# Similarity attention of layer 2: one run of intermediate products in front, then one block of eight groups with block-diagonal products

## The reference

```python
def _L2_gnn_ref(matrix, mask, adj, W):
    intermediate = jnp.einsum('bsh,hd->bsd', matrix, W)
    similarities = jnp.einsum('bsd,btd->bst', intermediate, matrix)
    similarities = similarities * adj
    key_mask = mask[:, None, :].astype(bool)
    masked = jnp.where(key_mask, similarities, NEG_INF)
    attn = jax.nn.softmax(masked, axis=-1)
    output = jnp.einsum('bst,bth->bsh', attn, matrix)
    return output
...
x = x + _L2_gnn_ref(_layernorm(x, axis=-1), nodemask, adj, L2_gnn_W)
```

## Time and profile before

| | us |
|---|---|
| median of 3 executions | 3874.0 (3872.6 to 3877.59) |
| the profiled execution | 3859.76 |
| its span, first to last instruction | 3857.9 |
| PE busy, PEld busy | 3137.0, 1980.1 |
| DVE busy, ACT busy, POOL busy | 2420.5, 1336.8, 234.5 |
| mean granted clock of PE, as a share of full speed | 0.871 |

### The profile page before, as it was taken

One profiled execution on the slowest core, in us unless ns is written; L12 is line 12 of the kernel. 1 busy time (PEld: TensorE's weight loads), 2 busy tenths in 40 slices (PEclk: granted clock), 3 DMA queues, 4 the chain that ended last, 5 costly groups with the idle time before them and its releaser, 6 DMA issues. The chain is left out here.

```text
span 3857.9 us, 56708 instructions
## 1 busy us (share of the span) xinstructions
PE 3137.0 (81%) x21385; PEld 1980.1 (51%) x21385; DVE 2420.5 (63%) x4174; ACT 1336.8 (35%) x2519; POOL 234.5 (6%) x196
## 2 busy tenths in 40 slices
PE   6357999999999999535549995789885988986998
PEld 5224555555555555324426663556552655653665
DVE  6636767777767776399673334488895345773333
ACT  3223434344434344110434443312111444543444
POOL 0000000000000000000000000033221004320000
PEclk7678999999999999755769997699997987897999
DMA  3121121112111112100013321000000212102322
GB/s 38 48 82 37 37 51 37 37 38 59 37 40 48 37 37 51 46 13 1 29 32 78 78 55 15 5 1 0 1 0 26 69 39 51 41 22 58 75 68 68
DMA packets 145000, 152.62 MB, mean 40 GB/s; under 512 B 66628, under 2 KB 124896, under 8 KB 142328
## 3 DMA queue, kind: packets, MB, share of 16 engines
q1 hardware_dynamic: 144800, 149.72, 16.0%
HBM read 141.26 MB, written 8.44 MB: 39 GB/s over the span
## 5 line engine op out<-in xcount | busy, mean ns | idle before, releaser
L812 DVE TENSOR_TENSOR f_hg<-f_hs,f_gb 128x640 f32<-128x640 f32 x320 | 263.7, 825 | 507.6 <-ACT f_hs L794 448.5
L2278 PE MATMUL hy_ps<-hy_uT,hy_win 128*128 128x512 f32 x1152 | 498.7, 594 | 0.0
L794 ACT ACTIVATE f_hs<-f_ph,f_b1t 128x320 f32<-128x320 f32 x640 | 335.1, 527 | 406.2 <-PE f_ph L762 402.2
L762 PE MATMUL f_ph<-XNP,f_w 128*128 (+1 forms) x1280 | 404.8, 440 | 12.9 <-PEq L644 8.6
L777 PE MATMUL f_po<-f_hg,f_w 128*128 128x320 f32 x1280 | 404.9, 439 | 8.9 <-DVE f_hg L812 8.9
L2278 PEld LDWEIGHTS hy_ps<-hy_uT,hy_win 128*128 128x128 f32 x1152 | 217.6, 190 | 281.2 <-issue 281.2
L762 PEld LDWEIGHTS f_ph<-XNP,f_w 128*128 128x128 f32 x1280 | 247.3, 194 | 117.5 <-issue 18.8
L777 PEld LDWEIGHTS f_po<-f_hg,f_w 128*128 128x128 f32 x1280 | 240.4, 191 | 126.4 <-issue 21.3
L2338 PE MATMUL hy_ps<-hy_wo,hy_yg 128*128 128x512 f32 x512 | 227.4, 603 | 0.0
L1803 PE MATMUL er_c<-XNG 128*128 128x400 f32 x544 | 204.6, 516 | 22.4 <-POOL XNG L1734 22.1
L1748 ACT ACTIVATE er_OT<-er_t 128x384 bf16<-128x384 f32 x128 | 61.1, 490 | 309.1 <-PE er_t L1773 309.1
(11 more groups left out here) (520 smaller groups left out, 5506.6 us busy)
## 6 DMA issues: line engine op xcount, KB each, us to landing
f_gb<-gate_rows SPq DMA_DIRECT2D x32, 1280.0 KB, 8.5
XNG<-hy_decays SPq DMA_DIRECT2D x32, 1024.0 KB, 9.5
hy_rb<-hy_inverse SPq DMA_DIRECT2D x128, 128.0 KB, 3.1
f_gb<-gate_rows SPq DMA_DIRECT2D x16, 640.0 KB, 5.1
g_KB<-g_keys SPq DMA_DIRECT2D x32, 320.0 KB, 4.5
hy_xn<-XNP SPq DMA_DIRECT2D x1, 4096.0 KB, 12.5
hy_XC<-hy_xn SPq DMA_DIRECT2D x16, 256.0 KB, 3.4
XNG<-in_L_ffn_edge_index_dram SPq DMA_DIRECT2D x2, 2048.0 KB
```

Source lines behind the costliest of these rows:

```text
L762: pe.matmul(psh[e % 2][k][:], w1[:, e, k * 128:(k + 1) * 128], chunk_view(g, c), start=True, stop=True).then_inc(h_ps, 1)
L794: ins = act.activation(hs[:, e % 2, k, :], psh[e % 2][k][:], ACT.Gelu, bias=b1t[:, e * H2 + k:e * H2 + k + 1])
L812: dve.tensor_tensor(hg[:, e % 2], hs[:, e % 2], gb[:, par, e, None, :].broadcast_to([128, H2, CH]), ALU.mult).then_inc(hg_ready, 1)
L2278: mm = pe.matmul(p[:], win[:, t, m * 128:(m + 1) * 128], uT[:, t, :], start=(t == 0), stop=(t == KT - 1))
```

## The change

The two blocks become one. The mask's 0/1 factor is multiplied into a product of mask and adjacency once (`key * adjG`), so that one multiplication out of PSUM applies both. PE makes all 16 intermediate products first, only their 320 real columns, and ACT keeps all of them in `inter` (128 x 128 x 40). Then PE, ACT and DVE go through eight groups of two chunks (`GC` = 2): in round k PE makes the scores of group k and, for group k - 2, turns the attention and makes the output products; DVE works out the softmax of group k in two parts (`shift`, `scale`) and between them adds the outputs of group k - 2 to `XT`. The turned tiles of a pair are copied to a block-diagonal `PT` (zeroed once by POOL), so that one product over 128 rows and 80 columns serves both graphs of a pair. The score products load 40 columns of weights in place of 64; the partitions in between are zeroed once in PSUM. The program of `l2_gnn` after the change (lines taken away are left out):

```diff
 
 def l2_gnn(nc, g):
 
+    GC = 2
+    GROUPS, GQ = NCH // GC, GC * CHP
     with nc.cleanup_on_exit(), ExitStack() as ctx:
         sb = lambda s, shape: ctx.enter_context(nc.sbuf_tensor(f"g2_{s}", shape, F32))
         sem = lambda s: nc.alloc_semaphore(f"g2_{s}")
...
+        w, inter = sb("w", [D, D]), sb("inter", [128, B, N])
         P, key, hide, st = sb("P", [128, PAIRS, N]), sb("key", [128, PAIRS, N]), sb("hide", [128, PAIRS, N]), sb("st", [128, PAIRS])
...
+        PT = sb("PT", [128, 2, CHP, 2, N])
+        bank = lambda s, shape: ctx.enter_context(nc.psum_tensor(f"g2_{s}", shape, F32))
+        psi, pss = [bank(f"i{i}", [128, CH]) for i in range(2)], [bank(f"s{i}", [128, CHP, N]) for i in range(2)]
+        pst, psz = [bank(f"t{j}", [128, CHP, N]) for j in range(2)], [bank(f"z{i}", [128, CH]) for i in range(2)]
+        w_in, key_in, blank, i_ps, i_out, s_ps, s_out, shifted, expd, attn, t_ps, t_out, z_ps, z_out = map(sem, (
+            "w_in", "key_in", "blank", "i_ps", "i_out", "s_ps", "s_out", "shifted", "expd", "attn", "t_ps", "t_out", "z_ps", "z_out"))
         block = ctx.enter_context(nc.Block())
+        group = lambda k: range(k * GC, (k + 1) * GC)
+
+        @block.sync
+        def _(sp):
+            sp.dma_start(w[:], g.L2_gnn_W).then_inc(w_in, 16)
+            masks = g.nodemask.rearrange("(q j) m -> j q m", j=2)
+            for j in range(2):
+                sp.dma_start(key[SLOT * j:SLOT * (j + 1), :, :], masks[j][None, :, :].broadcast_to([SLOT, PAIRS, N])).then_inc(key_in, 16)
+
+        @block.gpsimd
+        def _(pool):
+            pool.memset(PT[:], 0.0).then_inc(blank, 1)
 
         @block.tensor
         def _(pe):
...
+            def intermediate(c):
+                if c >= 2:
+                    pe.wait_ge(i_out, c - 1)
+                pe.matmul(psi[c % 2][:], w[:], g.XNP[:, c * CHG:(c + 1) * CHG, 0:N], start=True, stop=True).then_inc(i_ps, 1)
+
+            def scores(c):
+                if c >= 2:
+                    pe.wait_ge(s_out, c - 1)
+                for q in range(CHP):
+                    for j in range(2):
+                        mm = pe.matmul(pss[c % 2][rows(j), q, :], inter[:, c * CHG + 2 * q + j, :],
+                                       g.XNP[:, c * CHG + 2 * q + j, 0:N], start=True, stop=True)
+                mm.then_inc(s_ps, 1)
+
+            def turned(c):
                 if c >= 1:
...
+                    pe.wait_ge(t_out, c)
+                for q in range(CHP):
+                    for j in range(2):
+                        mm = pe.matmul(pst[j][rows(j), q, :], P[rows(j), c * CHP + q, :], g.ident[rows(j), rows(j)], start=True, stop=True)
+                mm.then_inc(t_ps, 1)
+
+            def product(c):
+                pe.wait_ge(t_out, c + 1)
+                if c >= 2:
+                    pe.wait_ge(z_out, c - 1)
+                for q in range(CHP):
+                    mm = pe.matmul(psz[c % 2][:, q * 2 * N:(q + 1) * 2 * N], g.XNG[:, c * CHP + q, :],
+                                   PT[:, c % 2, q].rearrange("p j n -> p (j n)"), start=True, stop=True)
+                mm.then_inc(z_ps, 1)
+
+            pe.wait_ge(w_in, 16)
+            for c in range(NCH):
+                intermediate(c)
+            pe.wait_ge(i_out, NCH)
+            pe.wait_ge(blank, 2)
+            for k in range(GROUPS + 2):
+                if k >= 2:
+                    pe.wait_ge(attn, k - 1)
+                for i in range(GC):
                     if k >= 2:
...
+                        turned((k - 2) * GC + i)
+                    if k < GROUPS:
+                        scores(k * GC + i)
+                    if k >= 2:
+                        product((k - 2) * GC + i)
 
         @block.scalar
         def _(act):
             for c in range(NCH):
...
+                act.wait_ge(i_ps, c + 1)
+                act.activation(inter[:, c * CHG:(c + 1) * CHG, :], psi[c % 2][:].rearrange("p (b n) -> p b n", n=N), ACT.Copy).then_inc(i_out, 1)
+            act.wait_ge(blank, 2)
+            for k in range(GROUPS + 2):
+                for i in range(GC):
+                    if k >= 2:
+                        c = (k - 2) * GC + i
+                        act.wait_ge(t_ps, c + 1)
+                        if c >= 2:
+                            act.wait_ge(z_ps, c - 1)
+                        for j in range(2):
+                            ins = act.activation(PT[rows(j), c % 2, :, j, :], pst[j][rows(j)], ACT.Copy)
+                        ins.then_inc(t_out, 1)
+                if k < GROUPS:
+                    act.wait_ge(shifted, k + 1)
+                    p = P[:, k * GQ:(k + 1) * GQ, :]
+                    act.activation(p, p, ACT.Exp).then_inc(expd, 1)
 
         @block.vector
         def _(dve):
...
+            part = lambda t, k: t[:, k * GQ:(k + 1) * GQ]
+            wide = lambda k: part(st, k)[:, :, None].broadcast_to([128, GQ, N])
+
+            def shift(k):
+                for c in group(k):
+                    dve.wait_ge(s_ps, c + 1)
+                    o = slice(c * CHP, (c + 1) * CHP)
+                    dve.tensor_tensor(P[:, o, :], pss[c % 2][:], key[:, o, :], ALU.mult).then_inc(s_out, 1)
+                dve.drain()
+                p = part(P, k)
+                dve.tensor_tensor(p, p, part(hide, k), ALU.add)
+                dve.drain()
+                dve.tensor_reduce(part(st, k), p, AX.X, ALU.max)
+                dve.drain()
+                dve.tensor_tensor(p, p, wide(k), ALU.subtract).then_inc(shifted, 1)
+
+            def scale(k):
+                p = part(P, k)
+                dve.wait_ge(expd, k + 1)
+                dve.tensor_reduce(part(st, k), p, AX.X, ALU.add)
+                dve.drain()
+                dve.reciprocal(part(st, k), part(st, k))
+                dve.drain()
+                dve.tensor_tensor(p, p, wide(k), ALU.mult).then_inc(attn, 1)
+
+            def add(k):
+                for c in group(k):
+                    dve.wait_ge(z_ps, c + 1)
+                    x = g.XT[:, c * CH:(c + 1) * CH]
+                    dve.tensor_tensor(x, x, psz[c % 2][:], ALU.add).then_inc(z_out, 1)
+
+            dve.memset(pss[0][:], 0.0)
+            dve.memset(pss[1][:], 0.0).then_inc(blank, 1)
+            dve.wait_ge(key_in, 32)
+            dve.tensor_scalar(key[:], key[:], 0.0, None, ALU.not_equal)
+            dve.drain()
+            dve.tensor_scalar(hide[:], key[:], 1.0, 1e30, ALU.subtract, ALU.mult)
+            dve.drain()
+            dve.tensor_tensor(key[:], key[:], g.adjG[:], ALU.mult)
+            dve.drain()
+            for k in range(GROUPS + 2):
+                if k < GROUPS:
+                    shift(k)
+                if k >= 2:
+                    add(k - 2)
+                if k < GROUPS:
+                    scale(k)
 
 
 def l3_gnn(nc, g):
```

More of the change, by code:

```diff
@@ L823, in l2_gnn @@
         sem = lambda s: nc.alloc_semaphore(f"g2_{s}")
-        w, inter = sb("w", [D, D]), sb("inter", [128, 2, CHG, SLOT])
+        w, inter = sb("w", [D, D]), sb("inter", [128, B, N])
         P, key, hide, st = sb("P", [128, PAIRS, N]), sb("key", [128, PAIRS, N]), sb("hide", [128, PAIRS, N]), sb("st", [128, PAIRS])
[L826 to L896, removed]
@@ L899, in l2_gnn @@
[L899 to L902, removed]
-        block = ctx.enter_context(nc.Block())
+        PT = sb("PT", [128, 2, CHP, 2, N])
+        bank = lambda s, shape: ctx.enter_context(nc.psum_tensor(f"g2_{s}", shape, F32))
@@ L906, in _ @@
         def _(pe):
[L907 to L915, removed]
-                if c >= 1:
-                    k = c - 1
-                    pe.wait_ge(t_out, k + 1)
-                    if k >= 2:
[L920 to L925, removed]
+            def intermediate(c):
+                if c >= 2:
+                    pe.wait_ge(i_out, c - 1)
+                pe.matmul(psi[c % 2][:], w[:], g.XNP[:, c * CHG:(c + 1) * CHG, 0:N], start=True, stop=True).then_inc(i_ps, 1)
@@ L937, in _ @@
         @block.vector
         def _(dve):
-            for c in range(NCH):
-                dve.wait_ge(z_ps, c + 1)
-                x = g.XT[:, c * CH:(c + 1) * CH].rearrange("p (q j n) -> p q j n", j=2, n=N)
-                for j in range(2):
-                    ins = dve.tensor_tensor(x[:, :, j, :], x[:, :, j, :], psz[c % 2][j][:], ALU.add)
-                ins.then_inc(z_out, 1)
+            part = lambda t, k: t[:, k * GQ:(k + 1) * GQ]
+            wide = lambda k: part(st, k)[:, :, None].broadcast_to([128, GQ, N])
```

## The result

| | before | after |
|---|---|---|
| median, 20 executions each | 3873.3 | 3860.0 |
| lowest to highest | 3857.5 to 3897.0 | 3839.6 to 3876.1 |
| the profiled execution | 3859.8 | 3839.6 |
| its span | 3857.9 | 3837.9 |
| this layer in it, first DMA to last addition | 100.4 | 79.8 |

The two medians differ by 13.3 us and the two means by 18.0; the ratio over the executions is 0.9951, with a 95% interval from 0.9932 to 0.9970, which on 3874 is 19 us less, between 12 and 26. It is faster, but the sum had 38.7. The executions of one and the same program differ by up to 40 us. How much of that lies in this layer isn't known, since each program has one profile; from program to program the span less the layer goes from 3748 to 3799. So a mechanism is read from the layer's length and clock in the profile, one execution each, and the timed ratios only say what a version is worth.

What follows compares the result with a forecast made beforehand. PE and DVE hardly ever worked together, much of PE's work at the low clock. Start 2369.1, plus 8.5, 23.3 and 10.2, gave 2411.1, with 2.5 for low clock 2413.6: 38.7 us saved, 3836, range 3825 to 3855.

Steps and rivals of the forecast that it cites:

- the sum: Whole layer at the high clock, with a low-clock ramp: end at 2413.6, 38.7 us earlier, time 3836; chance 0.66.
- the rival with the clock low: PE's clock stays low through all rounds: layer ends at 2429.6, 22.7 us saved, time 3851; chance 0.14.
- The start: Before the rounds: intermediate products hide behind the mask wait; first multiplication of scores at 2369.1, 17.3 us after the first DMA.
- DVE's price of a group: DVE's softmax and additions for one group: 4.4 us; the first two groups, without additions, 4.1 us each.
- a sign of error: Listed under what would show the prediction wrong: table loads standing before the exponentials; no size given.
- PE's price of a chunk: PE's scores, turning and output product for one chunk: 2.0 us at the high clock, 3.5 to 3.6 low.
- How they mesh: PE and DVE waiting on each other in the rounds: 4.65 us a group high; low, PE's own 7.2 sets it.
- the loop: DVE's second multiplication to first addition, then PE's product, turning and scores: 4.65 us a group at the high clock.
- Does the clock rise?: PE's clock in the rounds: 0.50 around rounds 1 to 3 and 1.00 after; high clock given 0.66.
- the ramp: Rounds 2 and 3 at the low clock after PE's near-idle gap: 1.0 + 1.5 = 2.5 us more.
- Changes of array shape: Rival: three array shapes a chunk cost 0.2 us each on top; 5 to 6 us less saved, 3841; chance 0.16.
- Slower through layer 3: Rival: the shift adds low-clock stretches in layer 3's attention, about 5.5 us each; eight more give 3879; chance 0.03.

Runs made afterwards that it cites:

- the filled runs: Changed kernel with extra 128 x 320 products in the two waits ahead of round 2: layer 78.5 us; with one more a chunk as well: 71.5 us.
- the run with both fillers: Changed kernel plus unread 128 x 320 products in the two waits ahead of round 2 and one behind each chunk's products from round 2: layer 71.5 us.

## Why the prediction was right or wrong

- **The time**: 3874.0 x 0.9951 is 3855, at the upper edge of the range from 3825 to 3855, and half of the 38.7 us saved in the sum. The sum had 3836 with the clock high; the range reached so far only because it took in the rival with the clock low, 3851. So it was the rival, with its chance of 0.14, that kept the time within the range; the time says nothing for the mechanism of the sum.
- **The start**: right. First multiplication at 17.7 us after the first DMA, forecast 17.3; the intermediate products done before it.
- **DVE's price of a group**: right to 0.05 us: 0.49 an instruction, 0.20 the reciprocal, 0.88 the two additions. The first two groups were to take 4.1 us each: the second took 4.0, the first 5.4, for the table load of 1.28. I named the table load as a sign of error and gave it no term; the order of ACT's waits was in the diff.
- **PE's price of a chunk**: near at the low clock (3.4, forecast 3.5 to 3.6), by two errors of opposite sign: the scores with 40 columns took 0.69 to 0.78 in place of 1.02, where I had put no saving, and the products 1.92 for 1.8. At the high clock the filled runs show 1.8 for 2.0: turning 0.43 (forecast 0.45), scores 0.42 (0.60), products 0.9 (0.95). That half the instructions save nothing at the low clock held.
- **How they mesh**: not tested at the high clock. No run holds it without 128 x 320 products in the rounds, so the 4.65 us of the loop was never seen; at the low clock PE's own work sets the round, 6.78 us for a forecast of 7.2.
- **"Does the clock rise?"**: the step that failed. I gave 0.66 to a rise within two rounds, and took 2.5 us for the ramp (by my own terms it is 2.3: 1.0 and half of 2.55); it never rose, and a round took 6.78 us in place of 4.65. The low-clock rival (0.14) has the mechanism and nearly the size: forecast 22.7 us saved, 20.6 in the profiled layer. Its terms: start of round 2 at 23.2 us for 21.4 (table load, exponential ahead of the copy), twelve chunks 42.4 for 43.2, tail 14.2 for 13.2. The gap that I cited for a low start was 6.07 us, not 5.6. The evidence was read too widely: both stretches that I cited for a rise contained 128 x 320 or 128 x 512 products, and those were just what the change moved out of the rounds to the front. The 0.50 of the second block and of the earlier trace rows was the nearer row.
- The Trainium skill, "TensorE: Matmul & The Clock Gate" (Why this matters for your kernels), has a TensorE that is kept busy back at its full clock. Here it was 95% busy for 42.4 us at 0.50, and with the extra product in each chunk 98% for 50 us: the trace disagrees again.
- **Changes of array shape**: did not show. Turning, scores and product follow each other with steps that their own work fills; behind a 128 x 320 pair, which takes 0.58 when another product follows (77.94 to 78.52 in layer 0), the turning starts 0.67 after the pair's first instruction (2388.50 to 2389.17 in the run with both fillers). The Trainium skill, "TensorEngine Tiling (Array Packing)" (Tiling Modes, Key Properties), speaks of a drain at such a change; by these rows it costs about 0.1 us.
- **Slower through layer 3**: not seen. From the layer's end to the end of the program the two profiled executions take 1405.6 us before and 1405.7 after. Between the profiles of all programs the time outside the layer moves by up to 51 us; what moves it was not looked into.

## What to carry to other kernels

Before moving large products out of a loop of small ones, ask which of them kept TensorE's clock up in the trace: the ones moved may have been paying for the others, as they did here. A wait or an idle slot of TensorE inside such a loop is the place for a product that is needed anyway, and if none is left, a useless one can be cheaper than the low clock: 8 us in the profiled layer here, though the timed executions don't show it. Price every version at both clocks, and give the row of the nearest mix, not of the nearest instruction, the greater weight.

## What the runs showed of the hardware

- A busy TensorE is not enough for the high clock: turning, scores, products and one 128 x 320 product a chunk, 98% busy, stayed at 0.50 for 50 us. Products of 128 x 80 on the whole array (streaming zeros), 88% busy, stayed at 0.50 for 25.8 us; with one 128 x 320 product to each eight instructions of them the clock rose within 6 us.
- Lifting and holding differ: that same mix, with one 128 x 320 product a chunk, stayed at 0.50 for 75 us when they began there, and at 1.00 for 46 us when they began there.
- The same instructions of this layer up to the same point kept 1.00 in one execution and fell to 0.50 in another, near a wait of 1.66 us.
- A table load can wait for what its activation waits for: 1.28 us that had been hidden came onto the path. That a second wait ahead of the activation brought this about fits all runs, and was not tested by itself.
